# Layer norm scaled on ScalarE with statistics taken at the result; squares on ScalarE; the split of the row maxima on VectorE

## The chip, the cores and the metric

The kernel runs on one core of a Trainium2 chip. The metric is the device time in microseconds (us) of that core, the median of several runs; lower is better. Five engines work from queues of their own, each in order: TensorE (PE), VectorE (DVE), ScalarE (ACT), GpSimd (POOL) and SyncE (SP), which here only issues DMAs. They synchronise by semaphores.

## What is computed

A hidden state of 4 batches x 1024 tokens x 512 channels passes four residual blocks, each fed by a layer norm. All blocks have causal attention with 16 heads of 32 channels, in float32:

```python
x = x + squared(_layernorm(x))   # normed features, scores squared
x = x + gated(_layernorm(x))     # top-1 gate picks one shared head for k, v; softmax
x = x + mqa(_layernorm(x))       # one key/value head for all queries; softmax
x = x + gated(_layernorm(x))
```

`_layernorm` subtracts the mean of the 512 channels of a token and divides by the square root of variance + 1e-5. In `squared`, queries and keys are themselves normed per head (their variance is the mean of squares of 32 centred channels) and the scores are squared and divided by their sum. In the softmax blocks a row maximum is subtracted.

## The kernel before

**Two programs.** The first does `squared` for four batches, the second the other three blocks for four batches: 4 + 12 stages, called `s`. A stage has 4 head groups (phases, `ph`) of 4 heads. A batch is 8 tiles of 128 tokens (`t`); scores are made in chunks of 512 queries (`c` = 0, 1) in ten bursts per phase (`keys`). The result of a block goes to DRAM and is loaded again as the next block's input, four stages later, and once more for the residual addition.

**One order for all.** `plan` (from L235) writes one list of events, and every engine walks it and does its own part of each event, so each queue is in this order. `spread` fills projection, transpose and output work between the score bursts of a phase by weight; an event with no weight costs nothing there. Work units of TensorE share two PSUM banks in turn (`free`, `wait_work`, `wait_free`), scores share three pairs of banks.

**Layer norm.** SP loads a tile into a ring of four (`load`, L619); the load of tile t+4 waits for the transpose of tile t. In `stats` DVE takes mean and variance (`bn_stats`, `bn_aggr`, two one-column operations, L884 to L887). POOL raises the variance to -0.5 (L654) and scales the tile in place (L656). In `ln` TensorE transposes it (L1139) and ACT evicts it (L758). `norm_events` (L92) sets this order, three tiles of statistics ahead.

**Output.** `rload` loads the old value into a ring of four `rest` tiles (L624), `out` transposes or projects the result. In gated stages DVE scales it by the inverse sums (L990), POOL adds it to `rest` (L745), SP stores (L632). In the other stages DVE adds it itself (L999).

**Maxima.** In the softmax stages TensorE also computes the scores row by row (`rows`, L1093), nine bursts per phase, one phase ahead; DVE reduces them (L862, and with the causal mask L867). After the third and the ninth burst comes `mxr`: DVE takes the negated maximum per query (L875, 128 x 16), POOL splits it into three bfloat16 terms whose sum is exact, by two subtractions and three copies (L697 to L701). `mxt` transposes them (L1197), ACT evicts them, and the key bursts add them in PSUM by a matmul (L1075) ahead of L1078. ACT takes the exponential (L775) or the scaled square (L781).

**POOL's other work.** It masks the diagonal blocks (L665) and adds the probabilities of all key blocks (`add`, L678 to L688) for the sums. In the squared stages it also squares keys and queries (`ksq` L721, `qsq` L728). The key squares go through a matmul (`kvar`, L1182), a DVE step and a power on POOL (L734) to the scale of L781.

## Time and profile before

| | |
|---|---|
| median of 3 runs | 4744.71 us (4744.14 to 4746.26) |
| profiled execution | 4741.89 us |
| its span, first to last instruction | 4740.1 us |
| granted TensorE clock, mean | 0.918 of full speed |
| busy: ACT, POOL | 1630.1 us (34%), 2991.2 us (63%) |

A page of the profile gives the busy time of each engine, then the span in 40 slices. Each digit below is the share of a slice in tenths; PEclk is the clock that TensorE was granted.

```profile
PE   6788888985978688688786888888798886977975
DVE  1212212222544444444444445444544444544452
ACT  1543444551223223323333333333233233232333
POOL 2967777983254646547676676776557466465587
PEclk9899998987989889899898999999899997988998
```

The first nine slices are the squared stages, with POOL at seven to nine tenths; the dip in the tenth is the change of programs. TensorE is the busiest engine throughout. In the timelines quoted further down a bracket gives the idle time of an engine before the instruction and who ended it.

### The profile page before, as it was taken

The page shows a single profiled execution, that of the slowest core. Times are in us where ns is not written, and L with a number is a line of the kernel's source. Part 1 is how long each engine was busy: PE and PEld are TensorE (multiplying, and loading weights), DVE is VectorE, ACT ScalarE, POOL GpSimd, SP SyncE. Part 2 cuts the span into 40 slices and gives each one's busy share as a digit, 9 for nine tenths or more (in the row PEclk, how much of TensorE's full clock was granted, in tenths as well). Part 3 has the DMA queues.
Part 4 walks back from the last instruction along what each step waited for, and adds up shares of the span by engine and source line. Part 5 has one row for each costly group of instructions (what it writes and reads, how often), then busy time and mean ns, then how long its engine had stood idle before and what let it go on. Part 6 is the DMA issues. An engine that isn't in the chain of part 4 may idle for free. (4 is left out here: it accounts for less than half of the span.)

```text
span 4740.1 us, 66857 instructions
## 1 busy us (share of the span) xinstructions
PE 3849.7 (81%) x26018; PEld 1585.2 (33%) x26018; DVE 1899.4 (40%) x4874; ACT 1630.1 (34%) x2433; POOL 2991.2 (63%) x2215
## 2 busy tenths in 40 slices
PE   6788888985978688688786888888798886977975
PEld 4343434322333233233232333333333332323332
DVE  1212212222544444444444445444544444544452
ACT  1543444551223223323333333333233233232333
POOL 2967777983254646547676676776557466465587
PEclk9899998987989889899898999999899997988998
DMA  1001010003000100100101010010001001010010
GB/s 62 18 1 37 18 36 19 19 19 103 18 1 1 54 1 8 48 1 21 34 17 38 1 34 21 23 32 25 30 1 54 1 19 36 1 53 2 1 37 27
DMA packets 63382, 115.05 MB, mean 24 GB/s; under 512 B 8672, under 2 KB 9184, under 8 KB 63072
## 3 DMA queue, kind: packets, MB, share of 16 engines
q1 hardware_dynamic: 63072, 110.77, 7.2%
q8 instruction: 212, 3.47, 0.3%
q14 instruction: 98, 0.80, 0.1%
HBM read 77.19 MB, written 33.55 MB: 23 GB/s over the span
## 5 line engine op out<-in xcount | busy, mean ns | idle before, releaser
L775 ACT ACTIVATE probs_soft<-banks 128x1024 f32<-128x1024 f32 (+1 forms) x960 | 848.6, 936 | 1426.0 <-PE banks L1078 1411.1
L688 POOL TENSOR_TENSOR added_soft<-added_soft,probs_soft 128x2048 f32<-128x2048 f32 (+3 forms) x384 | 1163.9, 3031 | 67.0 <-ACT probs_soft L775 47.9
L867 DVE CUSTOM_DVE_ANT_0 banks<-banks,mask 128x128 f32<-128x128 f32 (+3 forms) x1536 | 700.7, 525 | 739.1 <-PE banks L1093 739.1
L862 DVE TENSOR_REDUCE maxima_soft<-banks 128x2 f32<-128x1024 f32 x384 | 452.4, 1221 | 527.1 <-PE banks L1093 527.1
L1093 PE MATMUL banks<-k_soft,q_soft 32*128 32x512 f32 (+3 forms) x4608 | 531.4, 555 | 140.4 <-ACT probs_soft L775 140.3
L781 ACT ACTIVATE probs_squared<-banks,key_scale_squared 128x512 f32<-128x512 f32 (+3 forms) x768 | 379.2, 590 | 382.5 <-PE banks L1078 371.6
L665 POOL TENSOR_SCALAR_AFFINE_SELECT probs_soft<-probs_soft 128x512 f32<-128x512 f32 x384 | 239.7, 637 | 427.7 <-ACT probs_soft L775 427.6
L1078 PE MATMUL banks<-q_soft,k_soft 32*128 32x512 f32 (+3 forms) x4608 | 505.7, 521 | 0.0
L1131 PE MATMUL banks<-probs_soft,v_soft 128*32 128x512 f32 (+3 forms) x4608 | 454.2, 514 | 46.0 <-POOL probs_soft L665 31.7
L688 POOL TENSOR_TENSOR added_squared<-added_squared,probs_squared 128x2048 f32<-128x2048 f32 (+3 forms) x128 | 390.2, 3048 | 7.3 <-ACT probs_squared L781 1.9
L1075 PE MATMUL banks<-shift_soft,ones 32*128 32x512 bf16 (+3 forms) x2304 | 205.4, 344 | 227.2 <-DVE maxima_soft L867 136.4
L1093 PEld LDWEIGHTS banks<-k_soft,q_soft 32*128 32x128 f32 x4608 | 198.0, 199 | 378.6 <-issue 372.3
L681 POOL TENSOR_TENSOR added_soft<-probs_soft 128x2048 f32<-128x2048 f32 x48 | 216.8, 4518 | 123.0 <-ACT probs_soft L775 123.0
L1039 PE MATMUL banks<-xnT_soft,g_wq 128*128 128x512 f32 x512 | 254.9, 629 | 33.4 <-DVE scaled_out_soft L990 30.1
L1046 PE MATMUL banks<-g_wv,xnT_soft 128*128 128x512 f32 x512 | 247.9, 615 | 7.1 <-ACT k_soft L758 2.9
L1139 PE MATMUL banks<-ident,tiles_soft 128*128 128x128 f32 x384 | 81.2, 360 | 202.3 <-POOL tiles_soft L656 202.3
L1131 PEld LDWEIGHTS banks<-probs_soft,v_soft 128*32 128x32 f32 x4608 | 125.1, 112 | 353.7 <-issue 260.2
L1075 PEld LDWEIGHTS banks<-shift_soft,ones 32*128 32x128 bf16 x2304 | 64.9, 92 | 524.4 <-issue 505.0
L697 POOL CAST shift_cols_soft<-minus_max_soft 128x16 bf16<-128x16 f32 x96 | 24.4, 255 | 333.4 <-DVE minus_max_soft L875 333.4
L1078 PEld LDWEIGHTS banks<-q_soft,k_soft 32*128 32x128 f32 x4608 | 223.1, 195 | 25.6 <-issue 21.0
L1046 PE MATMUL banks<-g_wk,xnT_soft 128*128 128x512 f32 x512 | 223.8, 595 | 9.6 <-DVE picking_soft L846 9.6
L867 DVE DVE_READ_ACCUMULATOR2_ANT maxima_soft<- 128x1 f32 x1536 | 215.5, 140 | 0.0
(153 smaller groups left out, 4801.0 us busy)
## 6 DMA issues: line engine op xcount, KB each, us to landing
tiles_soft<-out SPq DMA_DIRECT2D x96, 256.0 KB, 2.9
rest_soft<-out SPq DMA_DIRECT2D x96, 256.0 KB, 3.0
out<-rest_soft SPq DMA_DIRECT2D x96, 256.0 KB, 2.1
tiles_squared<-in_x SPq DMA_DIRECT2D x32, 256.0 KB, 2.9
rest_squared<-in_x SPq DMA_DIRECT2D x32, 256.0 KB, 3.2
out<-rest_squared SPq DMA_DIRECT2D x32, 256.0 KB, 2.0
raw_wq<-in_squared_wq SPq DMA_DIRECT2D x1, 1024.0 KB, 5.6
raw_wk<-in_squared_wk SPq DMA_DIRECT2D x1, 1024.0 KB, 7.9
```

What stands on the lines that cost most here:

```text
L665: ins = pool.affine_select(out=cells, in_=cells, compare_op=ALU.is_ge, fill=0.0, base=0, pattern=[[0, HG], [1, P]], channel_multiplier=-1)
L688: ins = pool.tensor_tensor(sums, sums, slot(ph, n)[:, :, col:col + width], ALU.add)
L775: ins = act.activation(slot(ph, n)[:, 2 * a:2 * a + 2, 0:width], score_pair(e, a)[:, :, 0:width], ACT.Exp, scale=SCALE)
L781: ins = act.activation(slot(ph, n)[:, i, col:col + cols], score_pair(e, a)[:, x, col:col + cols], ACT.Square, scale=m["key_scale"][:, ph % ...
L862: ins = dve.reduce_max(m["maxima"][:, ph % 2, 2 * a:2 * a + 2, t, p], score_pair(e, a)[:, :, col:col + width], AX_X)
L867: ins = dve.tensor_tensor_reduce(scores, scores, k["mask"][:, CHUNK - width:CHUNK], 1.0, MASKED, ALU.add, ALU.max, m["maxima"][:, ph % 2, ...
L1039: ins = pe.matmul(out, wt[:, kc, cols], m["xnT"][:, kc, CHUNK * c:CHUNK * c + CHUNK], start=(kc == 0), stop=(kc == KC - 1))
L1046: ins = pe.matmul(out, m["xnT"][:, kc, P * t:P * t + P], wt[:, kc, cols], start=(kc == 0), stop=(kc == KC - 1))
L1075: pe.matmul(psum[:, score_bank(e, i), col:col + width], k["ones16"][D * i:D * i + D, :], m["shift"][D * i:D * i + D, ph % 2, c, q0:q0 + wi ...
L1078: ins = pe.matmul(psum[:, score_bank(e, i), col:col + width], k_of(ph)[D * i:D * i + D, P * kb:P * kb + P], m["q"][D * i:D * i + D, ph % N ...
L1093: ins = pe.matmul(psum[:, score_bank(e, i), col:col + P * blocks], m["q"][D * i:D * i + D, ph % NG, P * t:P * t + P], k_of(ph)[D * i:D * i ...
L1131: ins = pe.matmul(out[D * i:D * i + D, q0:q0 + width], left, slot(ph, n)[:, i, col:col + width], start=(x == 0), stop=(x == len(products) ...
```

## The change

Four steps of work move between engines, and one moves in time. The normalisation x * rstd + shift becomes one ACT activation per tile (`norm`), placed two tiles ahead of `ln`. The statistics of a tile of a later block are taken by DVE from the result in `rest` when it has been made (`ostat`, one tile behind `out`); they are kept for all batches, and POOL turns eight tiles at once into scale and shift (`oscale`). Only the first program still takes statistics of its own input from the loaded tile. SP's `rload` now also waits for `ostat` of the tile that the buffer held, and comes one tile later. Key and query squares go to ACT. The split of the maxima goes to DVE, right behind the maximum. POOL keeps additions, masks, powers and the copies. The core of the diff:

```diff
-def norm_events(s):
-
-    events = [("stats", s, t) for t in range(3)]
+def norm_events(kind, s):
+
+    lead = [("stats", s, t) for t in range(NT)] if kind == "squared" else []
+    events = lead[:3] + [("norm", s, t) for t in range(2)]
     for t in range(NT):
-        if t + 3 < NT:
-            events.append(("stats", s, t + 3))
+        events += lead[t + 3:t + 4]
+        if t + 2 < NT:
+            events.append(("norm", s, t + 2))
         events.append(("ln", s, t))
         if t + TILES < NT:
             events.append(("load", s, t + TILES))
     return events
+
+
+def out_events(kinds, s):
+
+    kept = kinds[s] == "squared" or s + B < len(kinds)
+    events = [("rload", s, t) for t in range(TILES)]
+    for t in range(NT + 1):
+        if t < NT:
+            events.append(("out", s, t))
+        if t:
+            if kept:
+                events.append(("ostat", s, t - 1))
+            if t - 1 + TILES < NT:
+                events.append(("rload", s, t - 1 + TILES))
+    return events + [("oscale", s)] * kept
...
+        outs = out_events(kinds, s - 1) if s else []
...
+        "stats": sb("stats", [P, 6]),
+        "mean_var": sb("mean_var", [P, 2]),
+        "minus_mean": sb("minus_mean", [P, B, NT]),
+        "var_eps": sb("var_eps", [P, B, NT]),
+        "rstd": sb("rstd", [P, B, NT]),
+        "shift": sb("norm_shift", [P, B, NT]),
...
+                    last = ("ostat", s, t - TILES) if t >= TILES else ("ostat", s - 1, t + TILES)
+                    if last in place:
+                        sp.wait_ge(sg.out_variance, place[last] + 1)
...
-                if u == "stats":
-                    _, s, t = e
-                    pool.wait_ge(sg.variance, place[e] + 1)
-                    then(pool.tensor_tensor(m["rstd"][:, t:t + 1], m["var_eps"][:, t:t + 1], k["minus_half"][:, 0:1], ALU.pow))
-                    x = m["tiles"][:, t % TILES, :]
-                    pool.tensor_scalar(x, x, m["minus_mean"][:, t:t + 1], m["rstd"][:, t:t + 1], ALU.add,
-                                       ALU.mult).then_inc(sg.normed, 1)
+                if u in ("stats", "oscale"):
+                    s = e[1]
+                    b = stages[s][1]
+                    some = slice(e[2], e[2] + 1) if u == "stats" else slice(0, NT)
+                    width = some.stop - some.start
+                    if u == "stats":
+                        pool.wait_ge(sg.variance, place[e] + 1)
+                    else:
+                        pool.wait_ge(sg.out_variance, place["ostat", s, NT - 1] + 1)
+                        pool.wait_ge(sg.normed, NT * (s + 1))
+                    then(pool.tensor_tensor(k["rstd"][:, b, some], k["var_eps"][:, b, some], k["minus_half"][:, 0:width], ALU.pow))
+                    pool.tensor_tensor(k["shift"][:, b, some], k["minus_mean"][:, b, some], k["rstd"][:, b, some], ALU.mult)\
+                        .then_inc(sg.scales_in if u == "stats" else sg.scales_out, 1)
...
-                elif u == "mxr":
-                    _, ph, c = e
-                    pool.wait_ge(sg.row_max, place[e] + 1)
-                    if place[e] >= NC:
-                        before = order["mxr"][place[e] - NC]
-                        wait_work(pool, ("mxt", before[1], before[2]))
-                    exact, cols, left = m["minus_max"][:, c], m["shift_cols"][:, c], m["rest_max"][:]
-                    then(pool.tensor_copy(cols[:, :, :, 0], exact))
-                    then(pool.tensor_tensor(left, exact, cols[:, :, :, 0], ALU.subtract))
-                    then(pool.tensor_copy(cols[:, :, :, 1], left))
-                    then(pool.tensor_tensor(left, left, cols[:, :, :, 1], ALU.subtract))
-                    pool.tensor_copy(cols[:, :, :, 2], left).then_inc(sg.max_split, 1)
-                    pool.wait_ge(sg.max_split, place[e] + 1)
...
-                elif u == "ksq":
...
-                    pool.tensor_tensor(m["key_square"][:, c], keys, keys, ALU.mult).then_inc(sg.key_squares, 1)
...
-                    pool.tensor_tensor(m["query_square"][:, c], queries, queries, ALU.mult).then_inc(sg.query_squares, 1)
...
+                elif u == "norm":
+                    _, s, t = e
+                    b = stages[s][1]
+                    act.wait_ge(sg.tile_in[t % TILES], DMA * (2 * s + t // TILES + 1))
+                    if not soft:
+                        act.wait_ge(sg.scales_in, place["stats", s, t] + 1)
+                    elif s >= B:
+                        act.wait_ge(sg.scales_out, s - B + 1)
+                    x = m["tiles"][:, t % TILES, :]
+                    act.activation(x, x, ACT.Identity, scale=k["rstd"][:, b, t:t + 1], bias=k["shift"][:, b, t:t + 1])\
+                        .then_inc(sg.normed, 1)
+                elif u == "ksq":
+                    _, ph, c = e
+                    wait_free(act, ("k2", ph, c))
+                    if ph:
+                        wait_work(act, ("kvar", ph - 1, c))
+                    act.activation(m["key_square"][:, c], k_of(ph)[:, CHUNK * c:CHUNK * c + CHUNK], ACT.Square)\
+                        .then_inc(sg.key_squares, 1)
...
+                    act.activation(m["query_square"][:, c], m["q"][:, ph % NG, CHUNK * c:CHUNK * c + CHUNK], ACT.Square)\
+                        .then_inc(sg.query_squares, 1)
...
+            def moments(x, b, t):
+
+                then(dve.bn_stats(k["stats"][:], x))
+                then(dve.bn_aggr(k["mean_var"][:], k["stats"][:]))
+                dve.tensor_scalar(k["minus_mean"][:, b, t:t + 1], k["mean_var"][:, 0:1], -1.0, None, ALU.mult)
+                return dve.tensor_scalar(k["var_eps"][:, b, t:t + 1], k["mean_var"][:, 1:2], EPS, None, ALU.add)
...
+                    then(dve.tensor_reduce(m["minus_max"][:, c].rearrange("p t i -> p i t"),
+                                      m["maxima"][:, ph % 2, :, TPC * c:TPC * c + TPC, 0:c + 1],
+                                           AX_X, ALU.max, negate=True))
                     if place[e] >= NC:
-                        dve.wait_ge(sg.max_split, place[e] - NC + 1)
-                    dve.tensor_reduce(m["minus_max"][:, c].rearrange("p t i -> p i t"),
-                                      m["maxima"][:, ph % 2, :, TPC * c:TPC * c + TPC, 0:c + 1],
-                                      AX_X, ALU.max, negate=True).then_inc(sg.row_max, 1)
+                        before = order["mxr"][place[e] - NC]
+                        wait_work(dve, ("mxt", before[1], before[2]))
+                    exact, cols, left = m["minus_max"][:, c], m["shift_cols"][:, c], m["rest_max"][:]
+                    then(dve.tensor_copy(cols[:, :, :, 0], exact))
+                    then(dve.tensor_tensor(left, exact, cols[:, :, :, 0], ALU.subtract))
+                    then(dve.tensor_copy(cols[:, :, :, 1], left))
+                    then(dve.tensor_tensor(left, left, cols[:, :, :, 1], ALU.subtract))
+                    dve.tensor_copy(cols[:, :, :, 2], left).then_inc(sg.max_split, 1)
+                    dve.wait_ge(sg.max_split, place[e] + 1)
...
-                    if s:
-                        dve.wait_ge(sg.normed, NT * (s - 1) + t + 1)
-                    x = m["tiles"][:, t % TILES, :]
-                    then(dve.bn_stats(m["stats"][:, t, :], x))
-                    then(dve.bn_aggr(m["mean_var"][:, t, :], m["stats"][:, t, :]))
-                    dve.tensor_scalar(m["minus_mean"][:, t:t + 1], m["mean_var"][:, t, 0:1], -1.0, None, ALU.mult)
-                    dve.tensor_scalar(m["var_eps"][:, t:t + 1], m["mean_var"][:, t, 1:2], EPS, None, ALU.add)\
-                        .then_inc(sg.variance, 1)
+                    moments(m["tiles"][:, t % TILES, :], stages[s][1], t).then_inc(sg.variance, 1)
+                    dve.wait_ge(sg.variance, place[e] + 1)
+                elif u == "ostat":
+                    _, s, t = e
+                    if kind_of(s) == "gated":
+                        dve.wait_ge(sg.summed, earlier("out", ("out", s, t), "gated") + 1)
+                    else:
+                        wait_free(dve, ("out", s, t))
+                    if not soft:
+                        dve.wait_ge(sg.scales_in, NT * (s + 1))
+                    elif s >= B:
+                        dve.wait_ge(sg.scales_out, s - B + 1)
+                    moments(m["rest"][:, t % TILES, :], stages[s][1], t).then_inc(sg.out_variance, 1)
+                    dve.wait_ge(sg.out_variance, place[e] + 1)
```

## Rows read from the trace of the kernel before

**Rows 1.** The page's part 1: busy us (share) and instructions of each engine.

```profile
PE 3849.7 (81%) x26018; PEld 1585.2 (33%) x26018; DVE 1899.4 (40%) x4874; ACT 1630.1 (34%) x2433; POOL 2991.2 (63%) x2215
```

**Rows 2.** Waits, engine PE: waiting line <- engine it waited for: total us, times, longest.

```profile
PE banks L1139 <- POOL tiles_soft L656: 202.3, 47, 30.8
...
PE banks L1075 <- DVE maxima_soft L867: 136.4, 128, 3.7
...
PE banks L1182 <- POOL key_square_squared L721: 52.2, 14, 7.7
...
PE banks L1131 <- POOL probs_squared L665: 33.7, 5, 12.0
...
PE banks L1039 <- DVE scaled_out_soft L990: 32.6, 5, 7.9
```

**Rows 3.** Waits, engine POOL (GpSimd): the wait ahead of the split.

```profile
POOL shift_cols_soft L697 <- DVE minus_max_soft L875: 333.4, 95, 26.8
```

**Rows 4.** Timeline at 1562 to 1575 us: start, duration, instruction, [idle before <- releaser].

```profile
1562.52 0.25 POOL L697 CAST shift_cols_soft<-minus_max_soft 128x16 bf16<-128x16 f32 x1 [4.56 <-DVE minus_max_soft L875]
...
1570.75 0.69 DVE L990 TENSOR_TENSOR scaled_out_soft<-banks,inverse_soft 128x512 f32<-128x512 f32 x1 [7.11 <-issue]
...
1574.36 3.78 PE L1039 MATMUL banks<-xnT_soft,g_wq 128*128 128x512 f32 x4 [7.95 <-DVE scaled_out_soft L990]
```

**Rows 5.** Timeline at 1933 to 1955 us: start of a stage's layer norm.

```profile
1933.48 13.78 SPq L619 DMA_DIRECT2D tiles_soft<-out  x8
...
1939.21 1.09 PE L1139 MATMUL banks<-ident,tiles_soft 128*128 128x128 f32 x4 [10.13 <-POOL tiles_soft L656]
...
1954.64 1.09 PE L1139 MATMUL banks<-ident,tiles_soft 128*128 128x128 f32 x4 [7.30 <-POOL tiles_soft L656]
```

**Rows 6.** Groups by form (busy us, mean ns), and a DMA issue (us to landing).

```profile
L656 POOL TENSOR_SCALAR tiles_soft<-tiles_soft,minus_mean_soft,rstd_soft 128x512 f32<-128x512 f32 x96 | 73.8, 768 | 10.0
...
L760 ACT ACTIVATE q_soft<-banks,bq 128x512 f32<-128x512 f32 x32 | 22.0, 688 | 85.8 <-PE banks L1039 85.8
...
tiles_soft<-out SPq DMA_DIRECT2D x96, 256.0 KB, 2.9
```

**Rows 7.** Timeline at 344 to 351 us: ScalarE, then TensorE's wait for key squares.

```profile
344.12 1.63 ACT L781 ACTIVATE probs_squared<-banks,key_scale_squared 128x256 f32<-128x256 f32 x4
...
350.61 1.62 PE L1182 MATMUL banks<-head_mean,key_square_squared 128*128 128x4 f32 x7 [6.50 <-POOL key_square_squared L721]
```

**Rows 8.** One stretch: us, busy us of each engine, granted clock, DMA share, GB/s.

```profile
1888.80:1899.00 10.20, 5.01 (x16) 1.84 (x16) 3.55 (x4) 0.00 (x0) 7.46 (x6) 0.50 0.39 128
```

**Rows 9.** One line each (duration ns min/median/max), then the timeline at 1394 us.

```profile
L961 DVE TENSOR_TENSOR y_squared<-y_squared,sums_squared x32: 691/693/4733, 151.4 to 1099.1; 128x512 f32<-128x512 f32 x32
...
L902 DVE TENSOR_SCALAR is_max_soft<-logits_soft x8: 226/940/3340, 1171.6 to 4355.6; 128x128 f32<-128x128 f32 x8
...
L886 DVE TENSOR_SCALAR minus_mean_soft<-mean_var_soft x96: 153/154/156, 1151.4 to 4264.5; 128x1 f32<-128x1 f32 x96
...
1394.54 3.34 DVE L902 TENSOR_SCALAR is_max_soft<-logits_soft 128x128 f32<-128x128 f32 x1
...
1397.92 1.37 DVE L904 TENSOR_TENSOR is_max_soft<-is_max_soft,rank 128x128 f32<-128x128 f32 x1
...
1394.33 3.47 POOL L679 TENSOR_TENSOR added_soft<-probs_soft 128x1536 f32<-128x1536 f32 x1
```

**Rows 10.** Timeline at 1313 to 1339 us: row maximum, split, adds, transpose, next scores.

```profile
1313.18 0.19 DVE L875 TENSOR_REDUCE minus_max_soft<-maxima_soft 128x16 f32<-128x32 f32 x1
...
1313.44 0.26 POOL L697 CAST shift_cols_soft<-minus_max_soft 128x16 bf16<-128x16 f32 x1 [2.10 <-DVE minus_max_soft L875]
...
1315.04 4.51 POOL L688 TENSOR_TENSOR added_soft<-added_soft,probs_soft 128x2048 f32<-128x2048 f32 x1
...
1316.36 0.61 PE L1197 MATMUL banks<-ident,shift_cols_soft 128*128 128x128 bf16 x4
...
1338.96 0.40 PE L1075 MATMUL banks<-shift_soft,ones 32*128 32x512 bf16 x4 [1.41 <-DVE maxima_soft L862]
```

More of the change, by code:

```diff
@@ L239, in plan @@
     first, rest = keys_and_values(kinds[0], 0)
-    events = [("load", 0, t) for t in range(TILES)] + norm_events(0) + first
+    events = [("load", 0, t) for t in range(TILES)] + norm_events(kinds[0], 0) + first
     if soft:
@@ L253, in plan @@
         halves = [h for g in range(NG) for h in phase(kinds, NG * s + g)]
-        outs = [("out", s - 1, t) for t in range(NT)] if s else []
-        if s:
-            outs = [("rload", s - 1, t) for t in range(TILES)] + [e for t in range(NT) for e in
-                                                                 [("out", s - 1, t)] + [("rload", s - 1, t + TILES)] * (t + TILES < NT)]
+        outs = out_events(kinds, s - 1) if s else []
         half = next((n for n, e in enumerate(outs) if e == ("out", s - 1, TPC)), 0)
@@ L267, in plan @@
             first, rest = keys_and_values(kinds[s + 1], s + 1)
-            work.append(([("load", s + 1, t) for t in range(TILES)] + norm_events(s + 1), 0, NG * HALVES))
+            work.append(([("load", s + 1, t) for t in range(TILES)] + norm_events(kinds[s + 1], s + 1), 0, NG * HALVES))
             work.append((first + rest, 2 * HALVES + 5, NG * HALVES))
@@ L272, in plan @@
     events += [("add", last, NKB - 1), ("av", last, "C"), ("sm", last, 1)] + [e for e, _ in sums_done(kinds[-1], last, 1)]
-    events += [("rload", stages - 1, t) for t in range(TILES)]
-    for t in range(NT):
-        events += [("out", stages - 1, t)] + [("rload", stages - 1, t + TILES)] * (t + TILES < NT)
+    events += out_events(kinds, stages - 1)
     return two_banks(events)
@@ L308, in __init__ @@
         self.variance = sem("variance")
+        self.scales_in = sem("scales_in")
+        self.out_variance = sem("out_variance")
+        self.scales_out = sem("scales_out")
         self.normed = sem("normed")
@@ L317, in __init__ @@
         self.maxima_ready = sem("maxima_ready")
-        self.row_max = sem("row_max")
         self.max_split = sem("max_split")
@@ L535, in act_program @@
     order = {name: [e for e in events if e[0] == name] for name in
-             ("load", "rload", "stats", "out", "mxr", "krep", "vst", "ksq", "qsq", "kvar", "nrm", "rs", "rw", "gate")}
+             ("load", "rload", "stats", "norm", "out", "ostat", "mxr", "krep", "vst", "ksq", "qsq", "kvar", "nrm", "rs", "rw", "gate")}
     order["picks"] = [e for e in events if e[0] in ("kall", "vall")]
@@ L643, in then @@
                 pool.wait_ge(sg.pool_step, steps.next())
-            if soft:
-                for c in range(NC):
-                    pool.memset(m["shift_cols"][:, c].rearrange("p t i d -> p (t i d)"), 0.0).then_inc(sg.cleared, 1)
-                pool.wait_ge(sg.cleared, NC)
             for e in events:
                 u = e[0]
-                if u == "stats":
-                    _, s, t = e
-                    pool.wait_ge(sg.variance, place[e] + 1)
-                    then(pool.tensor_tensor(m["rstd"][:, t:t + 1], m["var_eps"][:, t:t + 1], k["minus_half"][:, 0:1], ALU.pow))
-                    x = m["tiles"][:, t % TILES, :]
-                    pool.tensor_scalar(x, x, m["minus_mean"][:, t:t + 1], m["rstd"][:, t:t + 1], ALU.add,
-                                       ALU.mult).then_inc(sg.normed, 1)
+                if u in ("stats", "oscale"):
[11 more added lines that the diff above has]
+                        .then_inc(sg.scales_in if u == "stats" else sg.scales_out, 1)
                 elif u == "keys":
@@ L834, in then @@
                 dve.wait_ge(sg.vector_step, steps.next())
+            def moments(x, b, t):
[3 more added lines that the diff above has]
+                return dve.tensor_scalar(k["var_eps"][:, b, t:t + 1], k["mean_var"][:, 1:2], EPS, None, ALU.add)
+            if soft:
+                for c in range(NC):
+                    dve.memset(m["shift_cols"][:, c].rearrange("p t i d -> p (t i d)"), 0.0).then_inc(sg.cleared, 1)
+                dve.wait_ge(sg.cleared, NC)
             def each(x):
```

22 lines of the change are left out of this document (5 added, 17 removed).

## The prediction

> **What bounds the kernel now.** I read the page's busy line first [rows 1]: TensorE is busy for 3849.7 of 4740.1 us and VectorE for 1899.4, so the end is set by TensorE's stream and what interrupts it. Next I read who TensorE waits for [rows 2]. Of about 890 us without a matmul, GpSimd (POOL) owns the largest item, 202.3 us in the 47 waits for a normalised tile. It also owns 52.2 us for the key squares and 33.7 us for masks. VectorE (DVE) owns 136.4 us in 128 waits for score banks and 32.6 us in five waits for a bank of the output path. POOL itself stands idle for 333.4 us in front of the split of the row maxima, because its queue is in order and the split waits for DVE [rows 3]. Everything queued there starts late.
>
> The five output waits show this. POOL idles 4.56 us ahead of the split, the output adds behind it come late, DVE's third scaled output waits 7.11 us for a free buffer, and TensorE waits 7.95 us [rows 4]. The layer norm has the same shape. The load of stage 7's first tile is issued at 1933.48 and its transpose starts at 1939.21, 5.7 us later, after 10.13 us without work; some tiles later an add of 4.5 us, like the one in [rows 10], stands ahead of the scaling and TensorE waits 7.30 us [rows 5].
>
> **Layer norm and its statistics.** The change takes 128 scalings of 0.77 us from POOL and puts 128 Identity activations on ScalarE (ACT). For these I take 0.69 us, from the biased activation of the same shape [rows 6]. In the 12 soft stages the statistics are ready before, so the chain from load to transpose is 2.9 us of DMA, 0.69 of ACT and some 0.1 of handing over, 3.7 against 5.7. That is 2 us for each of 12 first tiles, 24 us. Seven stalls in the middle of a stage, of 5 to 7.3 us like the one in [rows 5], come from POOL's queue and go, 44 us. The smaller gaps among the other tiles, and the adds that reach the last output earlier, give some 22. Sum **90 us** of the 202.3; bounds 50 and 150. The cover now is the load itself: ACT's norm waits for its DMA, and queued behind it are evictions of scores and units, on which TensorE waits in turn. Norm t+2 is queued before the eviction of tile t while its load follows tile t-2, so a run of tiles keeps a cycle no longer than today's.
>
> **Squares.** 64 products leave POOL for ACT. In the case of [rows 7] ACT would be free for the key square at 345.75, where its score activations end, and done at about 346.4, while TensorE now waits until 350.61. That leaves about 2.3 of 6.50 us; over 14 waits I take **34 us** off 52.2, bounds 20 and 45. Masks in the squared stages gain from a shorter POOL queue: **10 us** of 33.7 (0 to 20).
>
> **Output waits.** With the split gone POOL can start its add 4.56 us earlier and drops 1.5 us of splitting itself. That is 6.1 us in each of five cases less the statistics now in DVE's path, **27 us** (0 to 33). SyncE's (SP's) reload of a result tile also moves one tile later, so its queue waits less for stores; that helps at the very end, and I count it at nothing.
>
> **Clock.** After such a stall TensorE is granted half speed, 1.2 GHz: 10.20 us at clock 0.50 with 5.01 us busy behind one of the five output waits [rows 8]. Half of that busy time is lost, 2.5 us; some 18 of the stalls above go entirely, **45 us** (20 to 80). All gains: 90 + 34 + 10 + 27 + 45 = **206 us**.
>
> **ACT and the moved statistics as costs.** ACT gets 128 x 0.69 and 64 of about the same, 130 us, at 34% use [rows 1]. Most falls into its waits; what stands ahead of a score eviction I put at 17 us (0 to 60). The statistics are the same number on DVE but now stand behind each output. In four gated stages they wait for POOL's sum of the tile before, with the next output and the row maxima queued behind; SP's reload waits for them too. They replace waits for DMA in the same queue. I take 18 us (0 to 60). POOL's twelve new scale computations wait for the last statistics of a stage; nothing on TensorE's path waits for these soon, and I cost them at nothing; the twelve waits on ACT for their results name scales of at least one stage earlier, except at the start of the second program, which a barrier covers. **35 us** together.
>
> **The split on VectorE.** This is the term that decides. Five operations of about 0.25 us replace POOL's five, 96 times. By themselves they fit: DVE idles ahead of most row reductions. But the trace shows what DVE does beside POOL [rows 9]. Its product of two SBUF tensors takes 691 ns and up to 4733; a one-input operation of 128 columns takes 226 ns and up to 3340; one of a single column never more than 156. The timeline shows how: L902 starts at 1394.54 and takes 3.34 us, until POOL's add of 1394.33 has ended at 1397.80; then POOL's next add has its turn, and L904, of 0.29 us by itself, takes 1.37. Where POOL has a queue, consecutive DVE operations each wait for one more POOL operation. The split is two two-input operations and three one-input copies of 16 columns. Today POOL stands still for it, so nothing collides; after the change the adds run.
>
> The second split of each phase shows the price [rows 10]. Its row maximum ends at 1313.4; POOL has been free for 2.0 us, so the 4.51 us add would run from 1311.3 to 1315.9. Then, one between each two DVE operations, come a mask of 0.6, adds of 3.5 and 1.3 and a mask of 0.6. If all five are held, the split ends 9.8 us after the maximum. TensorE reaches the transpose of these columns (L1197) at 1316.36, 3.0 us after the maximum. Over the 48 second splits this distance is under 3.3 us in 13, 4 to 8 in 24, longer in 11. Lateness: 13 x 7.3 + 24 x 3.7 = 184 us, less 1 us in each of 37 for the short waits it absorbs: 147. At half clock after the long ones: 30. First splits: the add of that half ends 0.95 us after the maximum and the next of 2.35 holds one operation, so the split ends at 4.6 us, where in 22 of 48 the next row reduction is due at 2.1 and TensorE already waits for it, by 1.41 us in [rows 10]: 22 x 2.2 = 48. Other DVE work directly behind a split: 30. Sum **255 us**. If only the two-input operations are held, the second split ends at 3.9 us: 13 x 1.4 = 18, first splits 30, others 40, sum 88. Unhindered the cost is near zero; if DVE also lost the turn in each alternation with further POOL work, it could reach 350. I take all five held, because the 128-column one-input operation is nearer in form to a 16-column copy than the single column is.
>
> Beside these rows: the Trainium skill, SBUF — State Buffer, section "Who interferes with whom", says the port pair is an exclusive lock, that a VectorE instruction with two SBUF inputs contends with a GpSimd one that reads SBUF, and that copies and casts can as well; the trace agrees for the two-input product (4733 ns) and for a one-input operation (3340 ns). The Trainium skill, VectorE: DVE Perf Modes, section "What auto-detection actually checks", puts a one-source SBUF operation of even extent into a two-port mode; no row here shows it for a strided 16-column copy. By that rule the sum is that of all five held.
>
> **The rivals.** The sum for the forecast: 4744.7 - 206 + 35 + 255 = **4829 us**, its own range 4745 to 4905. The profiled execution took 4741.89 us, 1.8 more than its span and 2.8 under the median, so I use the median. This forecast is already slower, so the first rival ends on the other side.
> Rival 1, only the two-input operations are held: 4744.7 - 206 + 35 + 88 = **4662**. For it: the copies are tiny and strided. Against: the one-input row.
> Rival 2, the adds end before the split or GpSimd yields, the split costs about 15: **4589**. For it: DVE idles, POOL is relieved. Against: POOL's 2.0 us lead over a 4.5 us add, the same in most phases.
> Rival 3, the gains and the lock cancel: the lateness is absorbed in the waits of 136.4 us which TensorE has on DVE anyway [rows 2], the split's cost near 170: **4744**.
> Rival 4, the change doesn't remove the norm's stalls, since ACT stands at its DMA wait with evictions behind: the gain of 90 and 15 of the clock fall away, 4829 + 105 = **4934**.
>
> **How the numbers follow.** Chances: forecast 0.47, rival 1 0.26, rival 2 0.11, rival 3 0.11, rival 4 0.05. A measurement of this kernel tells about 0.2% (9.5 us) from no change. Faster: rivals 1 and 2, 0.03 of rival 3 and 0.02 of the forecast's lower edge, 0.42. Same: 0.05. Slower: 0.53. The point between the signs: the splits must cost 206 - 35 = 171 us, 1.8 us each. The 8-in-10 range takes in rival 1 and most of the forecast, 4600 to 4890; I give 4825.
>
> **What would show it.** Right: DVE's L875-side split operations with medians far over 0.25 us and maxima near POOL's adds; TensorE's L1197 waiting for DVE, over 100 us in all; the normalised-tile wait of 202.3 near 110; the key-square wait under 25; POOL's 333.4 us gone. Wrong: split copies at 0.25 us throughout (then rival 1), two-input ones too (rival 2), or long ACT waits for DMA with TensorE waiting for scores (rival 4).

## The result

The changed kernel takes 4921.4 us (median of four runs, 4915.6 to 4933.0) where the kernel before takes 4744.4: 1.0376 times as long, 95% interval 1.0356 to 1.0396. It is slower by 177 us, and slower than the upper end of the forecast's range by 31.

The page of the profiled execution (4915.6 us), busy time of each engine, and one stretch of the trace that holds the end of a long stall and what follows (us, busy us of PE, PEld, DVE, ACT and POOL, granted clock, DMA share, GB/s):

```profile
PE 3898.4 (79%) x26018; PEld 1598.0 (33%) x26018; DVE 2373.7 (48%) x5356; ACT 1753.9 (36%) x2625; POOL 2688.5 (55%) x1501
...
1333.70:1343.90 10.20, 4.53 (x32) 1.88 (x36) 7.20 (x15) 1.22 (x2) 7.70 (x5) 0.50 0.00 0
```

Against [rows 1] POOL has lost 303 us of work, as meant, and ACT gained 124. DVE, which was given 96 small splits, has gained 474. TensorE (PE) runs the same 26018 matmuls and is busy for 49 us longer, because more of them run at half clock: the second row is such a stretch, clock 0.50 (1.2 GHz), around the end of a stall of 7.1 us. The rest of the 173 us of the span is idle time of PE. Whom it waits for:

```profile
PE banks L1241 <- DVE shift_cols_soft L914: 105.1, 20, 7.1
PE banks L1183 <- ACT tiles_soft L786: 98.5, 12, 30.5
PE banks L1273 <- DVE rest_soft L1043: 43.8, 7, 8.2
PE banks L1090 <- DVE picking_soft L876: 36.7, 10, 5.5
...
PE banks L1083 <- DVE y_soft L1024: 23.2, 3, 7.7
...
PE banks L1226 <- ACT key_square_squared L793: 16.6, 12, 2.8
...
PE banks L1083 <- DVE scaled_out_soft L1034: 12.8, 5, 3.2
```

The items of [rows 2] have gone the way the forecast said: tiles from 202.3 to 98.5 us (30.5 of it at the start of a program, as before), key squares from 52.2 to 16.6, the scaled output from 32.6 to 12.8. New are 105.1 us at the transpose of the split columns (L1197 before, L1241 now), and three waits for DVE that [rows 2] didn't have at this size: the output projection (L1273), the banks from which VectorE picks the gate's values (L1090), and a projection (L1083) whose bank is freed by VectorE's product into y. Behind the tiles stands a new wait of 19.6 us for ScalarE's evictions of them, so the idle time before their transposes fell from 202.3 to 119.1. The groups of DVE's split by form (busy us, mean ns of one), and the last copy by itself (ns, shortest, median and longest):

```profile
L912 DVE CAST shift_cols_soft<-rest_max_soft 128x16 bf16<-128x16 f32 x96 | 173.7, 1810 | 3.3
...
L910 DVE CAST shift_cols_soft<-minus_max_soft 128x16 bf16<-128x16 f32 x96 | 148.1, 1543 | 3.3
...
L913 DVE TENSOR_TENSOR rest_max_soft<-rest_max_soft,shift_cols_soft 128x16 f32<-128x16 f32 x96 | 89.5, 932 | 3.3
...
L911 DVE TENSOR_TENSOR rest_max_soft<-minus_max_soft,shift_cols_soft 128x16 f32<-128x16 f32 x96 | 51.6, 538 | 3.3
...
L914 DVE CAST shift_cols_soft<-rest_max_soft 128x16 bf16<-128x16 f32 x96 | 33.2, 346 | 3.3
...
L914 DVE CAST shift_cols_soft<-rest_max_soft x96: 202/203/2279, 1187.6 to 4844.5; 128x16 bf16<-128x16 f32 x96
```

Together 496 us for 480 operations whose shortest take 0.18 to 0.20 us each. The first four groups are far above that in the mean; the last copy (L914) is at 203 ns in the median, so it is held in a minority of the splits. Over all splits a second one of a phase takes 7.0 us in the mean from the maximum to the end, a first one 3.7. Here is one second split of a phase, the same place as in [rows 10]; PE's transpose of the columns is the last row:

```profile
1266.78 4.50 POOL L708 TENSOR_TENSOR added_soft<-added_soft,probs_soft 128x2048 f32<-128x2048 f32 x1
...
1268.65 0.19 DVE L903 TENSOR_REDUCE minus_max_soft<-maxima_soft 128x16 f32<-128x32 f32 x1
1268.87 2.47 DVE L910 CAST shift_cols_soft<-minus_max_soft 128x16 bf16<-128x16 f32 x1
...
1271.24 0.64 POOL L685 TENSOR_SCALAR_AFFINE_SELECT probs_soft<-probs_soft 128x512 f32<-128x512 f32 x1
1271.38 0.53 DVE L911 TENSOR_TENSOR rest_max_soft<-minus_max_soft,shift_cols_soft 128x16 f32<-128x16 f32 x1
...
1271.84 4.76 POOL L708 TENSOR_TENSOR added_soft<-added_soft,probs_soft 128x1536 f32<-128x1536 f32 x2
1271.94 3.37 DVE L912 CAST shift_cols_soft<-rest_max_soft 128x16 bf16<-128x16 f32 x1
1275.35 1.29 DVE L913 TENSOR_TENSOR rest_max_soft<-rest_max_soft,shift_cols_soft 128x16 f32<-128x16 f32 x1
1276.55 0.64 POOL L685 TENSOR_SCALAR_AFFINE_SELECT probs_soft<-probs_soft 128x512 f32<-128x512 f32 x1
1276.67 0.57 DVE L914 CAST shift_cols_soft<-rest_max_soft 128x16 bf16<-128x16 f32 x1
...
1277.39 0.58 PE L1241 MATMUL banks<-ident,shift_cols_soft 128*128 128x128 bf16 x4 [6.02 <-DVE shift_cols_soft L914]
```

Read POOL and DVE in pairs. The first copy starts at 1268.87 and ends at 1271.34, when POOL's add of 4.50 us has ended (1271.28). The subtraction lasts as long as the mask, the second copy as long as the add of 3.4 us (4.76 is two adds), the next subtraction as long as the second of them. The last copy lasts as long as the mask of 0.64 us beside it. The split takes 8.4 us from the maximum to the end; PE waits 6.02.

### The profile page after: what moved, and what is told of

Same layout as the page of the kernel before. It is cut to its first block, busy times and chain, and to the rows that moved or that the text cites. A ratio compares the mean times of both kernels' runs of the same rounds, so it can differ in the third digit from the quotient of the medians.

```text
span 4913.5 us, 66921 instructions
## 1 busy us (share of the span) xinstructions
PE 3898.4 (79%) x26018; PEld 1598.0 (33%) x26018; DVE 2373.7 (48%) x5356; ACT 1753.9 (36%) x2625; POOL 2688.5 (55%) x1501
## 4 chain that ended last, share of the span: by engine, by line
PE 43%; DVE 20%; ACT 5%; issue 4%; POOL 3%; DMA 1%; SPq 0%; POOLq 0%; DVEq 0%; ACTq 0%
PE banks L1137 9%; PE banks L1090 8%; PE banks L1175 7%; DVE banks L897 6%; PE banks L1122 6%; PE banks L1083 6%; ACT probs_soft L768 4%; DVE shift_cols_soft L912 3%; DVE shift_cols_soft L910 3%; PE banks L1119 2%; DVE maxima_soft L892 2%; PE banks L1273 2%; DVE rest_max_soft L913 2%; POOL added_soft L708 2%; DMA tiles_soft<-out 1%
## 5 line engine op out<-in xcount | busy, mean ns | idle before, releaser
L708 POOL TENSOR_TENSOR added_soft<-added_soft,probs_soft 128x2048 f32<-128x2048 f32 (+3 forms) x384 | 1162.6, 3028 | 83.8 <-ACT probs_soft L768 69.7
L892 DVE TENSOR_REDUCE maxima_soft<-banks 128x2 f32<-128x1024 f32 x384 | 452.5, 1221 | 461.0 <-PE banks L1137 460.3
L1119 PE MATMUL banks<-shift_soft,ones 32*128 32x512 bf16 (+3 forms) x2304 | 204.6, 343 | 251.1 <-DVE maxima_soft L897 125.8
L708 POOL TENSOR_TENSOR added_squared<-added_squared,probs_squared 128x2048 f32<-128x2048 f32 (+3 forms) x128 | 389.5, 3043 | 9.6 <-ACT probs_squared L774 3.2
L1090 PE MATMUL banks<-g_wv,xnT_soft 128*128 128x512 f32 x512 | 265.7, 652 | 41.3 <-DVE picking_soft L876 36.7
L1083 PE MATMUL banks<-xnT_soft,g_wq 128*128 128x512 f32 x512 | 257.7, 635 | 13.0 <-DVE scaled_out_soft L1034 9.8
L1090 PE MATMUL banks<-g_wk,xnT_soft 128*128 128x512 f32 x512 | 230.3, 611 | 17.3 <-DVE raw_logits_soft L936 17.3
L1122 PE MATMUL banks<-q_squared,k_squared 32*128 32x512 f32 (+3 forms) x1536 | 179.7, 553 | 19.7 <-ACT probs_squared L774 19.7
L1004 DVE RECIPROCAL sums_squared<-sums_squared 128x512 f32<-128x512 f32 x32 | 107.2, 3352 | 170.0 <-ACT sums_squared L753 140.6
```

The costliest lines, as they stand in the source:

```text
L708: ins = pool.tensor_tensor(sums, sums, slot(ph, n)[:, :, col:col + width], ALU.add)
L892: ins = dve.reduce_max(m["maxima"][:, ph % 2, 2 * a:2 * a + 2, t, p], score_pair(e, a)[:, :, col:col + width], AX_X)
L1083: ins = pe.matmul(out, wt[:, kc, cols], m["xnT"][:, kc, CHUNK * c:CHUNK * c + CHUNK], start=(kc == 0), stop=(kc == KC - 1))
L1090: ins = pe.matmul(out, m["xnT"][:, kc, P * t:P * t + P], wt[:, kc, cols], start=(kc == 0), stop=(kc == KC - 1))
L1119: pe.matmul(psum[:, score_bank(e, i), col:col + width], k["ones16"][D * i:D * i + D, :], m["shift"][D * i:D * i + D, ph % 2, c, q0:q0 + wi ...
L1122: ins = pe.matmul(psum[:, score_bank(e, i), col:col + width], k_of(ph)[D * i:D * i + D, P * kb:P * kb + P], m["q"][D * i:D * i + D, ph % N ...
```

## The experiments

Two theories. **A, the hold:** an operation of the split waits for whichever GpSimd operation runs, and the time that this takes out of VectorE's queue is the loss. **B, the rest:** a split in VectorE's queue costs whatever its length, or the moved statistics and ScalarE's norms cost what was not foreseen. All times are medians of four runs beside the kernel before on the same chip, which gave 4739 to 4742 us (4744 in the measurement of the change), so a difference between kernels measured apart is uncertain by some 5 us.

**The split as reductions.** A copy becomes a maximum over one element, a subtraction a sum over a pair:

```diff
-then(dve.tensor_copy(cols[:, :, :, 0], exact))
-then(dve.tensor_tensor(left, exact, cols[:, :, :, 0], ALU.subtract))
...
+then(dve.tensor_reduce(cols[:, :, :, 0], first[:, :, :, 0:1], AX_X, ALU.max))
+then(dve.tensor_reduce(first[:, :, :, 1], cols[:, :, :, 0:1], AX_X, ALU.max, negate=True))
+then(dve.tensor_reduce(second[:, :, :, 0], first[:], AX_X, ALU.add))
...
```

> The changed kernel, but each of VectorE's two subtractions and three copies of 16 columns is written with tensor_reduce: a copy is the maximum over one element, a subtraction the sum over a pair of which the second is stored negated (six reductions for five operations, same result). TensorE's work, the queues and their order are those of the changed kernel. No reduction in the changed kernel's trace is longer than its shortest by over 10 ns, so: if the port lock makes the loss (A), the six take 0.17 to 0.2 us each, a second split 1.2 us in place of 8.4, the 117 us of TensorE at the transpose of these columns go, with most of the 140 us of late DVE evictions behind the splits, 20 at the shifts and some 50 of half clock: 4600 us (4560 to 4660). If the loss comes from the split standing in VectorE's queue at all, or from the moved statistics (B), it stays over 4850.

Measured 4585.8 us, 0.9675 of before (0.9661 to 0.9690). The same place in its timeline, and PE's group of the columns' transposes (busy us, mean ns, idle before it):

```profile
1264.88 4.51 POOL L709 TENSOR_TENSOR added_soft<-added_soft,probs_soft 128x2048 f32<-128x2048 f32 x1
...
1266.97 0.23 DVE L911 TENSOR_REDUCE shift_cols_soft<-pairs_soft 128x16 bf16<-128x16 f32 x1
...
1268.13 0.22 DVE L917 TENSOR_REDUCE shift_cols_soft<-pairs_soft 128x16 bf16<-128x32 f32 x1
...
1269.40 0.60 PE L1244 MATMUL banks<-ident,shift_cols_soft 128*128 128x128 bf16 x4
...
L1244 PE MATMUL banks<-ident,shift_cols_soft 128*128 128x128 bf16 x384 | 41.0, 234 | 1.6 <-DVE scaled_out_soft L1037 0.8 <-ACT xnT_soft L752 0.6
```

The same add of 4.5 us runs over the whole split, and no reduction waits for it: six take 0.18 to 0.23 us each, and the split ends 1.4 us after the maximum, ahead of PE. The 117.1 us that PE idles before these transposes in the changed kernel are 1.6 here. B falls: the split stands in the same place of the same queue, and statistics, norms and squares are those of the change. This kernel beats both others, by 3.2% and 6.8%. The 10 ns that the expectation names are exceeded by one group, the row maxima at L892, which take 1215 to 1228 ns in the changed kernel; that is no hold.

**The split back on GpSimd**, the rest of the change kept (the old code in POOL's queue, `row_max` restored).

> The changed kernel with the split put back on GpSimd, everything else of the change kept. A (lock): the loss of the splits goes, GpSimd's idling ahead of the split comes back and with it some 30 us of output waits and 20 of masks: 4640 us (4590 to 4690). B (the moved statistics and ScalarE's norms cost what was not foreseen): it stays over 4744, about 4820.

Measured 4625.4 us, 0.9754 (0.9736 to 0.9772). So the two other parts of the change (norm with statistics, and squares) are worth 114 us without the third.

**Only the split moved**, in the kernel before.

> The kernel before with nothing but the split moved to VectorE. A (lock): the whole loss shows with none of the gains, the transpose's wait 100 to 130 us, evictions behind the splits 100 to 150, half clock 50: 5030 us (4970 to 5100). B: the split is cheap, 4700 to 4800. A third reading, that the collisions come only because the change relieves GpSimd's queue, gives 4800 to 4900 here: with norms and squares still on GpSimd fewer splits would meet an add.

Measured 5033.3 us, 1.0623 (1.0607 to 1.0638). PE's waits:

```profile
PE banks L1192 <- DVE shift_cols_soft L871: 105.1, 20, 7.1
...
PE banks L1224 <- DVE rest_soft L994: 43.0, 7, 8.2
PE banks L1041 <- DVE picking_soft L833: 36.6, 10, 5.5
```

105.1, 43.0 and 36.6 us, the three waits of the changed kernel to within 1 us. The split's move by itself costs 294 us, and relieving GpSimd by the other parts plays no role in these waits.

**GpSimd stands still for the split**, in the changed kernel:

```diff
+elif u == "mxr":
+    pool.wait_ge(sg.max_split, place[e] + 1)
```

> The changed kernel with one wait added: GpSimd, where its split stood in the kernel before, waits until VectorE has split. No GpSimd operation then runs beside the five. A (lock): each of the five is at its shortest time, 0.18 to 0.20 us, a second split 1.1 us; GpSimd idles over 300 us ahead of this wait as before; 4630 us (4580 to 4690). B: as the changed kernel, over 4850.

Measured 4628.1 us, 0.9772 (0.9752 to 0.9792). With the same five forms on DVE and nothing on GpSimd beside them, the copy that took 1810 ns in the mean and the subtraction of 932 are:

```profile
L914 DVE CAST shift_cols_soft<-rest_max_soft 128x16 bf16<-128x16 f32 x96 | 19.5, 203 | 3.3
...
L915 DVE TENSOR_TENSOR rest_max_soft<-rest_max_soft,shift_cols_soft 128x16 f32<-128x16 f32 x96 | 17.8, 185 | 3.3
```

This is the direct proof of the hold: nothing but GpSimd's running beside was taken away. The price is that GpSimd stands idle for these splits, and the kernel comes out where the split on GpSimd itself does.

**Which of the five are held.** First the copies alone as reductions, subtractions as they are:

> The changed kernel with the three copies of the split as reductions and the two subtractions as they are, so only two-input operations can be held: rival 1 as a kernel. If each operation that can be held waits for about one GpSimd operation and the copies were half of the holding (A), a second split takes 2.6 us until the add of 4.5 us ends, the second subtraction meets the next one: 3.4 to 4 us in place of 8.4, and 40 to 70 us over the kernel with all five as reductions: 4640 us (4610 to 4680). If the subtractions alone make the loss, since each still waits for a whole add (C), near 4850.

Measured 4667.8 us, 0.9845 (0.9829 to 0.9861). The same place again:

```profile
1264.36 4.51 POOL L708 TENSOR_TENSOR added_soft<-added_soft,probs_soft 128x2048 f32<-128x2048 f32 x1
...
1266.72 2.20 DVE L911 TENSOR_TENSOR rest_max_soft<-minus_max_soft,shift_cols_soft 128x16 f32<-128x16 f32 x1
...
1268.82 0.63 POOL L685 TENSOR_SCALAR_AFFINE_SELECT probs_soft<-probs_soft 128x512 f32<-128x512 f32 x1
...
1269.20 0.29 DVE L913 TENSOR_TENSOR rest_max_soft<-rest_max_soft,shift_cols_soft 128x16 f32<-128x16 f32 x1
```

Then the subtractions as reductions, copies as they are:

> The other half: the three copies stay copies, the subtractions become reductions. A (one-input copies are held as two-input operations are): copy one is held to the end of the 4.5 us add, copy two for the 3.4 us of the next, copy three for the 1.3 us of the one after, a second split 7.5 to 8 us, 4860 us (4800 to 4910). If copies of 16 columns are short by themselves and only late behind the subtractions (rival 1's view): near 4600, all copies at 0.20 us.

Measured 4871.6 us, 1.0264 (1.0247 to 1.0281). Its three copies:

```profile
L911 DVE CAST shift_cols_soft<-pairs_soft 128x16 bf16<-128x16 f32 x96 | 149.3, 1555 | 3.9 <-DVE pairs_soft L905 0.7
...
L914 DVE CAST shift_cols_soft<-pairs_soft 128x16 bf16<-128x16 f32 x96 | 140.0, 1459 | 3.3
...
L917 DVE CAST shift_cols_soft<-rest_max_soft 128x16 bf16<-128x16 f32 x96 | 94.7, 987 | 3.3
```

Both kinds are held. Alone the subtractions cost 82 us over the kernel with reductions, the copies 286. The subtraction meets one whole add (2.20 us, to the end of the one begun at 1264.36) and then only the rest of the short mask (0.29 us, to the mask's end); of three copies, with reductions between them, each can meet another operation, and all three groups are far over 0.20 us in the mean. Both times lie in their expected ranges; the first kernel is 82 us over the kernel with reductions where 40 to 70 were expected. The two together make 368, the five in one kernel 336; why not the same wasn't looked into.

**Time alone, without a hold.** Is the loss only the time that VectorE is away? A reduction of a constant, which nothing uses, is put into the middle of each split:

```diff
+held = 5 if c == 0 else 11
...
+then(dve.tensor_reduce(m["padding"][:, 0:held],
+     k["mask"][:, None, :].broadcast_to([P, held, CHUNK]), AX_X, ALU.max))
```

> The kernel with the split as reductions and, in the middle of each split, one more reduction of a constant on VectorE that nothing uses: over 5 x 512 elements in a first split of a phase and 11 x 512 in a second, some 2.7 and 5.9 us, so that the splits last about as long as in the changed kernel (3.7 and 7.0 us in the mean), but without a hold on the port. If the loss of the changed kernel is the time that VectorE is taken out of its queue, whatever takes it (A), 4910 us (4850 to 4950), with 90 to 120 us of TensorE's waits at the transpose of the columns and 110 to 150 behind the splits in VectorE's other evictions. If part of the loss is what the lock does to GpSimd or to others (D), under 4830.

> As the padded kernel, but with the padding of 2.7 us in the first split of each phase alone. The forecast gave the first splits 48 us of lateness at the next row reduction, and part of 30 elsewhere: 4640 us (4615 to 4670). Rival: VectorE's evictions behind a first split are as exposed as those behind a second: 4690 or more.

Measured 4940.1 us, 1.0420 (1.0404 to 1.0436), and with the first splits alone 4692.4 us, 0.9898 (0.9883 to 0.9913). The padding by form, and PE's waits in the padded kernel:

```profile
L918 DVE TENSOR_REDUCE padding_soft<-mask 128x11 f32<-128x5632 bf16 x48 | 289.0, 6020 | 1.6
...
L918 DVE TENSOR_REDUCE padding_soft<-mask 128x5 f32<-128x2560 bf16 x48 | 135.4, 2821 | 1.6
...
PE banks L1248 <- DVE shift_cols_soft L921: 85.9, 21, 6.2
PE banks L1280 <- DVE rest_soft L1050: 49.7, 7, 8.2
PE banks L1097 <- DVE picking_soft L878: 39.8, 10, 9.3
```

A padding takes 2.82 us in a first and 6.02 us in a second split in every phase, so it is not held. The padded kernel comes close to the changed one (105.1, 43.8 and 36.7 there) with 45 us more of VectorE's time, so D falls: no effect of the lock on others is needed. The first splits alone cost 107 us where the forecast gave them 48 and a part of 30; the rival of that run was right. The table sets the busy time of the split's operations, 96 splits summed from the groups by form, against the loss; both are counted over the kernel with reductions (117 us, 4585.8 us).

| kernel | DVE time added | time lost | lost per us |
|---|---|---|---|
| copies reduced | 139 us | 82 us | 0.59 |
| padding in first splits | 135 | 107 | 0.79 |
| subtractions reduced | 337 | 286 | 0.85 |
| the change (all five held) | 379 | 336 | 0.89 |
| padding in both | 424 | 354 | 0.83 |

VectorE is busy for 44% of the span in the kernel with reductions, and yet 0.6 to 0.9 of every microsecond added at this place is lost.

**What the other parts are worth.** Squares put back on GpSimd, in the kernel with reductions:

> The kernel with the split as reductions, but key and query squares back on GpSimd. The forecast's term: the key squares' wait returns by 34 us and with it some 8 of half clock, less nearly nothing of ScalarE's cost: 4625 us (4605 to 4650). Rival: with GpSimd's queue now free of the split, its squares come in time, and moving them was worth nothing: 4586 (4575 to 4600).

Measured 4638.7 us, 0.9770 (0.9745 to 0.9796): the squares are worth 53 us, and GpSimd without the split does not bring them in time by itself.

Statistics taken late, from the loaded tile, in all stages, the norm still on ScalarE:

```diff
-    lead = [("stats", s, t) for t in range(NT)] if kind == "squared" else []
+    lead = [("stats", s, t) for t in range(NT)]
...
-    kept = kinds[s] == "squared" or s + B < len(kinds)
+    kept = False
```

> The kernel with the split as reductions, but in all stages the statistics taken after the tile's load, VectorE before the norm, and none behind the outputs; ScalarE still scales. If early statistics carry part of the norm's gain (the forecast counts 24 us at the first tiles, and the cycle in a run of tiles grows by VectorE's and GpSimd's 2 us): 4640 us (4610 to 4680). Rival: the statistics behind the outputs cost what they bring (8 us of waits for y, 10 at the output projection): 4585 (4570 to 4600).

Measured 4673.9 us, 0.9855 (0.9840 to 0.9870), 88 us over the kernel with early statistics.

The kernel before with the split as reductions, and the same with the squares on ScalarE:

> The kernel before with the split alone moved to VectorE, as reductions: what the move is worth without a hold. GpSimd's 333 us ahead of the split go, so its masks, output adds and norms come earlier: forecast's terms 27 and 10 for outputs and masks, some 30 of the norm's, and some 15 of half clock: 4665 us (4640 to 4700). Rival: GpSimd's idling ahead of the split was cover for nothing on TensorE's path: 4740.

> The same with the squares on ScalarE too, so only the norm and its statistics stay as in the kernel before. The squares give 53 us, as in the kernel with them put back; 4612 us (4590 to 4640), and the norm's move is then worth what is left to the 4586 us of the kernel with all three, some 25. Rival: the squares give less once GpSimd is free of the split: 4640 or more, and the norm 60.

Measured 4689.0 us, 0.9892 (0.9876 to 0.9909), and 4640.1 us, 0.9788 (0.9767 to 0.9808). So, added one after the other to the kernel before: the split away from GpSimd without a hold gives 51 us, the squares 49, and the norm with early statistics 54. The norm is worth more than the 25 us expected there, the split's move less than the 74. The second kernel stands at its rival's 4640, but not for the rival's reason: the squares give 49 of the 53 us, and the kernel that they were added to was itself 24 us above its forecast. Late statistics (4673.9) stand above even the kernel with the norm on GpSimd (4640.1): ScalarE's wait ahead of its norm, PE's waits for the tiles, and PE's group of the scores behind ScalarE:

```profile
ACT tiles_soft L786 <- POOL norm_shift L679: 218.5, 62, 56.5
...
PE banks L1187 <- ACT tiles_soft L786: 126.7, 11, 30.5
...
L1141 PE MATMUL banks<-k_soft,q_soft 32*128 32x512 f32 (+3 forms) x4608 | 537.2, 560 | 158.7 <-ACT probs_soft L771 158.6
```

62 waits for GpSimd's scales in place of 28 for the load (129.3 us in the kernel with reductions), 126.7 us of PE's waits for the tiles and 42.5 for their evictions in place of 104.9 and 19.5, and 158.7 us in front of the scores in place of 144.3. That evictions queue behind the waiting norm is the likely reason for these; it wasn't followed wait by wait. PE is also busy for 39 us longer for the same matmuls (3851.5 against 3812.5). The move to ScalarE pays only together with the early statistics.

## Why the prediction was wrong

The sign and the mechanism were right. The failed step is the size of the lateness: the forecast's sum for the held splits, 255 us, is 336. Within it the term "other DVE work directly behind a split: 30" measured 117, and the 30 us for half clock measured 86; the two terms that were counted from rows came out smaller than forecast.

- **All five held**: chosen for the one-input operation of 128 columns in [rows 9], confirmed for the copies as a kind; the fifth operation is over 0.25 us in 31 of 96 splits only, and in first splits mostly the first operation alone is held. The forecast's 9.8 us for a second split is 8.4 in the one shown; it went by the same alternation, operation by operation, but added some 0.25 us for each operation on top of its hold. L902 in [rows 9] ends 0.08 us after the add that holds it, so the durations add up to 8.5. Rival 1 was also run, as a kernel: 4667.8 us for its 4662. Rival 2 is the kernel with reductions, 4585.8 for its 4589; its six operations are unhindered. Rivals 3 and 4 don't hold: the 136.4 us of [rows 2] that rival 3 meant to absorb the lateness are still 125.8 us, so they took in 11 at most; and with the norm on ScalarE the stalls in the middle of a stage are gone, against rival 4.
- **PE at the transpose of the columns**: forecast 147 us, measured 115.5 (117.1 less 1.6). The form differs too: 105.1 us of it are 20 waits of 5.3 us in the mean, where the forecast had 37 late splits. **Row reductions behind first splits**: forecast 48 (its own 4.6 less 2.1 us in 22 cases gives 55), measured 31 (PE's idle time before the shifts, 251.1 against 220.5). A first split ends at 3.7 us in the mean and not at 4.6.
- **"Other DVE work directly behind a split: 30"**: this term failed. No row was counted for it, nor for the 30 us of half clock. Measured by PE's idle time before each group, changed kernel against reductions: the gate's values 41.3 against 10.5, the output projection 44.4 against 14.5, the queries of `m_wq` 38.5 against 10.4, and four smaller ones, 117 us in all. One case, with the end of the split ahead of it:

```profile
2886.58 3.37 DVE L912 CAST shift_cols_soft<-rest_max_soft 128x16 bf16<-128x16 f32 x1
...
2891.54 0.69 DVE L1043 TENSOR_TENSOR rest_soft<-banks,rest_soft 128x512 f32<-128x512 f32 x1
...
2892.28 2.07 PE L1273 MATMUL banks<-m_wo,y_soft 128*128 128x512 f32 x2 [8.06 <-DVE rest_soft L1043]
```

  DVE's addition of 0.69 us at L1043 frees the bank that the output projection wants, and stands behind the held split: PE waits 8.06 us. VectorE's queue is in order, and every bank that it empties is late by what the split is late. The forecast followed the transposes and the row reductions and left the rest of the queue to a round number.
- **Clock**: forecast 30 us for the long lateness, measured 86 (PE busy 3898.4 against 3812.5 for the same matmuls, mean granted clock 0.909 against 0.936). The likely reason is the same: the stalls of 4 to 8 us at other lines, which the sum didn't see, come on top of those at the transpose. The lost clock wasn't counted stall by stall. The four terms: 115.5 + 31 + 117 + 86, less some 16 that other waits give back, are the 334 us by which the spans differ.
- **The gains** were right in sum: 206 less 35 of costs less 15 for an unhindered split gives 156; the kernel with reductions is 153 under the kernel before. That they agree so closely is in part luck, since their parts shift and the costs weren't measured apart. The forecast's 34 us and their clock for the squares are 49 to 53. Its 90 us for the norm are a decrease of 77 in [rows 2]'s largest item, of which 40 come already with the split gone from GpSimd (162.7 us left in that kernel), less 12 at the first program's tiles. The chain of a first tile is close to what was worked out, 3.8 us where its parts were followed: 2.8 from the load's issue to the norm, 0.81 of ScalarE (0.69 was taken from another operation), 0.14 to the transpose. The output waits fell from 33.4 to 12.7, 21 us for 27. The clock gave 37 for 45.
- **The moved statistics**, priced as a cost of 18 us, turned out to be what makes the norm's move pay.
- **The range** reached to 4890 and should have reached further: the forecast's own range ended at 4905, still below the 4921. Its note that the lock could cost 350 comes near the 336 by luck: the reason given there, that VectorE would lose its turn to further POOL work, does not show in the split above, where each operation waits for one POOL operation.

The Trainium skill, SBUF — State Buffer, section "Who interferes with whom", lets copies, casts and one-source scalar operations in two-port modes, and operations with two SBUF inputs, contend with GpSimd, and excludes those with one input outside these modes. All runs agree: copies (up to 3.52 us, in the kernel with subtractions reduced) and subtractions (up to 3.34) are held, reductions to 16 columns (0.23 at most) never.

## What to carry to other kernels

Before small work moves to VectorE beside a busy GpSimd, look for its form in the trace: the longest duration of such an operation, not its median, says whether it is held, and consecutive held operations can each pay one GpSimd operation. Where a form is held, write it in another one: here six reductions of 117 us in all do the work of five held operations of 496. And price a delay in an in-order queue by everything that stands behind it, bank by bank; VectorE's 44% of busy time gave no sign of it here.

## What was not expected

That reductions do the work of copies and subtractions at next to no cost (117 us for all 576 against 94 for 480 copies and subtractions with GpSimd standing still): the prediction had no such kernel in it. One of the six over all 96 splits (duration in ns, shortest, median and longest), with and without an operation of GpSimd beside it:

```profile
L911 DVE TENSOR_REDUCE shift_cols_soft<-pairs_soft x96: 221/224/229, 1184.6 to 4508.7; 128x16 bf16<-128x16 f32 x96
```

And no hold of GpSimd by the split shows: GpSimd's additions at L708 take 3028 ns in the mean in the changed kernel, and 3031 in the kernel before, where nothing of the split ran beside them. VectorE's operations of the split are 0.2 us long by themselves; whether a long one would hold GpSimd was not run.
